# Attention with divided heads, turned logits and more sums on TensorE in a fused cross-attention and mixture-of-experts kernel

## What is computed

```python
# B, N, D = 8, 512, 512; context of M = 1601 rows; 16 heads of 32
q = qdq(layernorm(x)) @ qdq(wq).T + bq;  k, v = split(ctx @ wkv.T + bkv)
attn = softmax(q @ k.T / sqrt(32))            # per batch and head, 512 x 1601
o = attn @ v
x = x + tanh(g_xattn) * (qdq(o) @ qdq(wp).T + bp)
h = layernorm(x)
logits = h @ gate_w.T                         # 32 experts
# top 4 of the 32 within the best 2 of 4 groups, weights from sigmoid(logits), capacity 2*(N*K/E)
shared = (silu(h @ shared_gate) * (h @ shared_up)) @ shared_down
x = x + tanh(g_ffn) * (experts(h) + shared)
```

## Time and profile before

| | |
|---|---|
| median of 3 runs | 3153.32 us (3148.29 to 3154.59) |
| profiled execution | 3147.53 us, its span 3145.8 us |
| TensorE busy | 90% of the span |
| VectorE, ScalarE, GpSimd busy | 57%, 44%, 57% |
| attention | to about 2457 us of the span |
| shared FFN and routing | to about 2903 us |
| experts | the rest |

### The profile page before, as it was taken

One profiled execution on the slowest core, in us unless ns is written; L12 is line 12 of the kernel. 1 busy time (PEld: TensorE's weight loads), 2 busy tenths in 40 slices (PEclk: granted clock), 3 DMA queues, 4 the chain that ended last, 5 costly groups with the idle time before them and its releaser, 6 DMA issues. The chain is left out here.

```text
span 3145.8 us, 43433 instructions
## 1 busy us (share of the span) xinstructions
PE 2824.6 (90%) x14876; PEld 1215.4 (39%) x14876; DVE 1791.0 (57%) x3878; ACT 1383.7 (44%) x2460; POOL 1808.2 (57%) x1570
## 2 busy tenths in 40 slices
PE   5898999899989988999899899989998799998987
PEld 3333333333333333333333333333332354444766
DVE  6576567756675666667557756775664343433222
ACT  4155446644564456456545644564456210000111
POOL 0285567656656676667566656765668423223455
PEclk9798999999999999999999999999999899899999
DMA  4111012101211031103111201221011123131996
GB/s 126 39 45 52 24 35 72 54 22 35 77 53 39 18 94 47 35 22 95 30 35 58 66 23 35 72 54 33 23 53 57 68 99 110 61 121 55 310 282 116
DMA packets 146586, 215.59 MB, mean 69 GB/s; under 512 B 24984, under 2 KB 78232, under 8 KB 146368
## 3 DMA queue, kind: packets, MB, share of 16 engines
q1 hardware_dynamic: 130496, 195.95, 20.7%
q0 software_dynamic: 15872, 16.87, 2.9%
HBM read 126.49 MB, written 34.24 MB: 51 GB/s over the span
## 5 line engine op out<-in xcount | busy, mean ns | idle before, releaser
L1549 POOL TENSOR_TENSOR prob_acc<-prob_acc,probs 128x512 f32<-128x512 f32 x1152 | 1430.7, 1279 | 420.6 <-ACT probs L1065 420.6
L1065 ACT ACTIVATE probs<-s_ps 128x512 f32<-128x512 f32 (+1 forms) x1664 | 937.2, 596 | 770.0 <-PE s_ps L841 738.8
L1286 DVE TENSOR_REDUCE piece_max<-r_all 128x1 f32<-128x400 f32 (+1 forms) x2048 | 1027.7, 565 | 142.1 <-PE r_all L763 135.3
L763 PE MATMUL r_all<-k_flat,q_stack 96*128 96x400 f16 (+1 forms) x2048 | 604.7, 352 | 110.2 <-DVE piece_max L1286 41.4
L841 PE MATMUL s_ps<-q_stack,k_flat 97*128 97x512 f16 (+1 forms) x1664 | 631.1, 396 | 60.7 <-ACT probs L1065 52.5
L855 PE MATMUL o_ps<-probs,v_sb 128*32 128x512 f32 (+1 forms) x3328 | 465.3, 632 | 21.6 <-ACT probs L1065 21.6
L841 PEld LDWEIGHTS s_ps<-q_stack,k_flat 97*128 97x128 f16 (+1 forms) x1664 | 160.1, 101 | 630.5 <-ACT probs L1065 424.5
L1546 POOL COPY prob_acc<-probs 128x512 f32<-128x512 f32 x128 | 73.0, 616 | 494.1 <-PE sum_ps L875 359.5
L763 PEld LDWEIGHTS r_all<-k_flat,q_stack 96*128 96x128 f16 x2048 | 203.7, 100 | 387.7 <-DVE piece_max L1286 125.8
L1581 POOL DMA_INDIRECT slot_rows<-payload,slot x128 | 125.7, 982 | 300.1 <-DVE slot L1462 230.7
L1280 DVE SCALAR_TENSOR_TENSOR k_lo<-r_all,bk_col,k_hi 128x400 f16<-128x400 f32 (+1 forms) x128 | 81.7, 638 | 280.7 <-ACT k_hi L1023 280.7
(11 more groups left out here) (220 smaller groups left out, 2832.3 us busy)
## 6 DMA issues: line engine op xcount, KB each, us to landing
k_flat<-k_hi SPq DMA_DIRECT2D x256, 100.1 KB, 2.2
ctx_raw<-in_ctx SPq DMA_DIRECT2D x96, 256.0 KB, 2.8
xin<-in_x SPq DMA_DIRECT2D x16, 1024.0 KB, 5.6
k_flat<-k_lo SPq DMA_DIRECT2D x128, 100.1 KB, 2.2
v_sb<-in_L_ffn_w SPq DMA_DIRECT2D x18, 512.0 KB
q_stack<-q_hi SPq DMA_DIRECT2D x256, 32.0 KB, 1.8
h_rows<-work SPq DMA_DIRECT2D x8, 1024.0 KB, 4.5
x_rows<-xin SPq DMA_DIRECT2D x8, 1024.0 KB, 6.8
```

The source lines that it names most:

```text
L763: last = nc.tensor.matmul(ps[:, 0:w], q_stack[0:KSPLIT, g % 2, j, qt * P:(qt + 1) * P], k_stack[0:KSPLIT, g % 2, j, at:at + w], start=True ...
L1065: nc.scalar.activation(probs[0:w, slot, j, :], s_ps[j % SBANKS][0:w, :], ACT.Exp).then_inc(probs_ready, 1)
L1286: V.reduce_max(piece_max[:, j * TT + qt, i:i + 1], ps[:, 0:PIECE[i]], X_AXIS).then_inc(free_of(*key), 1)
L1549: last = G.tensor_tensor(prob_acc[:, j, :], prob_acc[:, j, :], probs[:, slot, j, :], ALU.add)
```

## The change

Three things change.

- **The division.** `copy_sums` and the tile `sumT` go. Behind the tiles of step 0 of the next group VectorE takes the reciprocal of `sum_ps` as it stands, 128 x 512, into `sum_sb`, and multiplies ScalarE's copy of the heads by it in place (`divide_heads`). The turn of the heads waits for that; what is turned is copied into `work` by one instruction. ScalarE's copy of the next group's heads waits until the turn of these is done.
- **The logits.** The 32 columns of the gate are the weights and the four row tiles of h move, into four strips of 32 partitions of one bank (tile `logitsT`). ScalarE copies them to SBUF, and one transpose turns them back (tile `logits`). The second down tile stands between the two.
- **The last group's sums.** TensorE sums the steps 2, 4, 6, 8, 10 and 12 of the last group, GpSimd adds the other 7.

`add_bias` stays at step 4 of g = 0. The core of the diff:

```diff
@@ -41,8 +41,8 @@
 SBANKS, NBANKS, HALVES = 2, 4, 3
-POOL_STEPS = [kt for kt in range(KT) if kt not in (4, 8, KT - 1)]
-FIRST_SUMS = 4
+PE_SUMS, LAST_PE_SUMS = (4, 8, KT - 1), (2, 4, 6, 8, 10, KT - 1)
+BIAS_STEP = 4
 MAX_STEPS = range(3, KT - 1)
@@ -74,9 +74,24 @@
+def pe_sums(n):
+
+    return PE_SUMS if n + 1 < B * GROUPS else LAST_PE_SUMS
+
+
+def pool_steps(n):
+
+    return [kt for kt in range(KT) if kt not in pe_sums(n)]
+
+
+def added_after(n):
+
+    return sum(len(pool_steps(m)) for m in range(n))
+
+
 def adds_before(s):
-    return (s // KT) * len(POOL_STEPS) + POOL_STEPS.index(s % KT)
+    return added_after(s // KT) + pool_steps(s // KT).index(s % KT)
@@ -159,8 +174,8 @@
     if f + 1 < B:
-        order += [("hT", f + 1, c) for c in range(DC)] + down[0:1] + [("logits", f + 1)]
-        down = down[1:]
+        order += [("hT", f + 1, c) for c in range(DC)] + down[0:1] + [("logitsT", f + 1)] + down[1:2] + [("logits", f + 1)]
+        down = down[2:]
     return order + down
@@ -332,6 +346,7 @@
         top8 = v_sb[:, 11, 0:TT * E].rearrange("p (t q e) -> p t q e", t=TT, q=EGROUPS)
+        logits_sb = sb("logits_sb", [P, P], FP32)
         gsum = sb("gsum", [P, TT, 8], FP32)
@@ -767,16 +783,10 @@
                 elif kind == "oT":
-                    pe.wait_ge(heads_copied, group(b, key[2]) + 1)
+                    pe.wait_ge(heads_divided, group(b, key[2]) + 1)
                     ps = open_tile(*key)
...
                         last = nc.tensor.transpose(ps[:, t * P:(t + 1) * P], oT_sb[:, t * P:(t + 1) * P], ident[:, :])
-                elif kind == "sumT":
-                    pe.wait_ge(sums_copied, group(b, key[2]) + 1)
-                    ps = open_tile(*key)
-                    for t in range(TT):
-                        last = nc.tensor.matmul(ps[:, t * GH:(t + 1) * GH], sum_sb[:, t * P:(t + 1) * P],
-                                                ident[:, ::DH], start=True, stop=True)
                 elif kind == "oiT":
@@ -795,14 +805,18 @@
                         last = nc.tensor.transpose(ps[:, t * P:(t + 1) * P], h_in[b % 2][:, t, c * P:(c + 1) * P], ident[:, :])
-                elif kind == "logits":
+                elif kind == "logitsT":
                     for c in range(DC):
...
                     ps = open_tile(*key)
-                    for t in range(TT):
-                        for c in range(DC):
-                            last = nc.tensor.matmul(ps[:, t * E:(t + 1) * E], hT[:, c, t * P:(t + 1) * P], gateT[:, c, :],
+                    for c in range(DC):
+                        for t in range(TT):
+                            last = nc.tensor.matmul(ps[t * E:(t + 1) * E, 0:P], gateT[:, c, :], hT[:, c, t * P:(t + 1) * P],
                                                     start=(c == 0), stop=(c == DC - 1))
+                elif kind == "logits":
+                    wait_read(pe, "logitsT", b)
+                    ps = open_tile(*key)
+                    last = nc.tensor.transpose(ps[:, 0:TT * E], logits_sb[:, :], ident[:, :])
                 elif kind in ("gate", "up"):
@@ -854,23 +868,24 @@
                                             probs[0:w, slot, j, :], start=(kt == 0), stop=(kt == KT - 1))
-                if kt in POOL_STEPS:
+                if kt in pool_steps(s // KT):
                     last.then_inc(probs_used, 1)
...
                 w, slot = rows(kt), s % HALVES
-                if kt == FIRST_SUMS and s >= KT:
-                    pe.wait_ge(sums_copied, s // KT)
+                first = kt == pe_sums(s // KT)[0]
+                if first and s >= KT:
+                    pe.wait_ge(sums_inverted, s // KT)
                 for j in range(GH):
                     last = nc.tensor.matmul(sum_ps[j * DH:(j + 1) * DH, :], ones[0:w, :], probs[0:w, slot, j, :],
-                                            start=(kt == FIRST_SUMS), stop=False)
+                                            start=first, stop=False)
                 last.then_inc(probs_used, 1)
...
-                pe.wait_ge(probs_added, (n + 1) * len(POOL_STEPS) * GH)
+                pe.wait_ge(probs_added, added_after(n + 1) * GH)
                 for j in range(GH):
@@ -1039,6 +1054,9 @@
                     nc.scalar.copy(hT[:, key[2], :], ps[:, :]).then_inc(free_of(*key), 1)
+                elif kind == "logitsT":
+                    ps = full(act, *key)
+                    nc.scalar.copy(logits_sb[:, :], ps[:, 0:P]).then_inc(free_of(*key), 1)
                 elif kind == "logits":
@@ -1067,12 +1085,10 @@
                 act.wait_ge(probs_used, (n + 1) * KT)
+                if n:
+                    act.wait_ge(bank_full[ring.last_bank("oT", (n - 1) // GROUPS, (n - 1) % GROUPS)],
+                                ring.done("oT", (n - 1) // GROUPS, (n - 1) % GROUPS))
                 nc.scalar.copy(oT_sb[:, :], o_ps[:, :]).then_inc(heads_copied, 1)
-
-            def copy_sums(n):
-
-                act.wait_ge(acc_summed, n + 1)
-                nc.scalar.copy(sum_sb[:, :], sum_ps[:, :]).then_inc(sums_copied, 1)
@@ -1095,8 +1111,6 @@
                         tile(key)
-                if kt == 0 and s:
-                    copy_sums(s // KT - 1)
                 if g == 2 and b + 1 < B:
@@ -1305,33 +1318,35 @@
                 po = full(dve, "oT", b, g)
-                pss = full(dve, "sumT", b, g)
-                V.reciprocal(rsum[:, :, :].rearrange("p t j -> p (t j)"), pss[:, 0:TT * GH]
-                             ).then_inc(free_of("sumT", b, g), 1)
-                wait_read(dve, "sumT", b, g)
-                for t in range(TT):
-                    last = V.tensor_tensor(
-                        work[:, t, g * P:(g + 1) * P].rearrange("p (j d) -> p j d", j=GH),
-                        po[:, t * P:(t + 1) * P].rearrange("p (j d) -> p j d", j=GH),
-                        rsum[:, t, :].unsqueeze(2).to_broadcast([P, GH, DH]), ALU.mult)
-                    if t < TT - 1:
-                        step.mark(last)
-                last.then_inc(free_of("oT", b, g), 1)
+                V.tensor_copy(work[:, :, g * P:(g + 1) * P], po[:, :].rearrange("p (t n) -> p t n", t=TT)
+                              ).then_inc(free_of("oT", b, g), 1)
                 wait_read(dve, "oT", b, g)
+
+            def divide_heads(n):
+
+                dve.wait_ge(acc_summed, n + 1)
+                V.reciprocal(sum_sb[:, :], sum_ps[:, :]).then_inc(sums_inverted, 1)
+                dve.wait_ge(sums_inverted, n + 1)
+                dve.wait_ge(heads_copied, n + 1)
+                V.tensor_tensor(oT_sb[:, :], oT_sb[:, :], sum_sb[:, :], ALU.mult).then_inc(heads_divided, 1)
...
             for b, g, kt in steps():
+                s = step_of(b, g, kt)
                 for key in lead_tiles(b, g, kt) + fill_tiles(b, g, kt):
                     tile(key)
+                if kt == 0 and s:
+                    divide_heads(s // KT - 1)
                 if g == 2 and b + 1 < B:
...
                     h_part(b - 1, kt)
+            divide_heads(B * GROUPS - 1)
             heads_out(B - 1, GROUPS - 1)
@@ -1559,9 +1574,9 @@
             for b, g, kt in steps():
-                if kt in POOL_STEPS:
+                if kt in pool_steps(group(b, g)):
                     add_probs(step_of(b, g, kt))
-                elif g == 0 and kt == FIRST_SUMS and b:
+                if g == 0 and kt == BIAS_STEP and b:
                     add_bias(b - 1)
```

More of the change, by code:

```diff
@@ L94, in head_tiles @@
 def head_tiles(b, g):
-    return [("oT", b, g), ("sumT", b, g)]
+    return [("oT", b, g)]
 def lead_tiles(b, g, kt):
@@ L179, in __init__ @@
             order += lead_tiles(*at) + fill_tiles(*at)
-        order += head_tiles(B - 1, GROUPS - 1) + [("hT", 0, c) for c in range(DC)] + [("logits", 0)]
+        order += head_tiles(B - 1, GROUPS - 1) + [("hT", 0, c) for c in range(DC)] + [("logitsT", 0), ("logits", 0)]
         for f in range(B):
@@ L319, in build @@
         prob_acc = sb("prob_acc", [P, GH, N], FP32)
-        rsum = sb("rsum", [P, TT, GH], FP32)
         hT, actT = probs[:, 0], probs[:, 1]
@@ L447, in build @@
         heads_copied = sem("heads_copied")
-        sums_copied = sem("sums_copied")
+        sums_inverted = sem("sums_inverted")
+        heads_divided = sem("heads_divided")
         h_ready = sem("h_ready")
@@ L894, in _ @@
                         heads_of(s - 1)
-                if kt and (kt - 1) not in POOL_STEPS:
+                if kt and (kt - 1) not in pool_steps(s // KT):
                     sums_of(s - 1)
@@ L902, in _ @@
             accumulated_sums(B * GROUPS - 1)
-            for key in head_tiles(B - 1, GROUPS - 1) + [("hT", 0, c) for c in range(DC)] + [("logits", 0)]:
+            for key in head_tiles(B - 1, GROUPS - 1) + [("hT", 0, c) for c in range(DC)] + [("logitsT", 0), ("logits", 0)]:
                 tile(key)
@@ L1061, in exp_of @@
                     act.wait_ge(probs_used, before + 1)
-                if before >= 0 and before % KT in POOL_STEPS:
```

(8 more changed lines are left out.)

## The result

The changed kernel takes 3200.03 us (median of 4 runs, 3198.85 to 3201.55) against 3150.81 for the kernel before: 1.0157, 95% interval 1.0135 to 1.018. It is slower, by 49 us. The profiled execution took 3198.85 us (span 3197.1), 17 us above the 3181.5 that the sum gave for it. The table has the time by stage, from the first matmul of each in the two profiles. (The last group's q tile is made at the start of the group before it, so the second stage holds two groups.)

A forecast was written before the change was run, and what follows sets the result against it. TensorE, busy 90% of the span, was taken as the bound. From the profiled 3147.5 us, +28 - 21 - 5 + 32 = +34 gave 3181.5; the forecast was 3184, range 3141 to 3212 (3168 to 3198 by itself).

The forecast's parts named there:

- the rival of 3205: Each new stand of TensorE brings its clock down to 1.2 GHz for a while: +24 us, 3205; chance 0.20.
- the two waits that it named: ScalarE's square root some 4 us later in seven groups; TensorE idle about 4.5 before each later batch's third down tile.
- The reciprocal: VectorE's reciprocal of 512 elements a partition, out of PSUM, takes 3.25 us, with a 0.69 us multiply behind it.
- The statistics behind the division: In g = 1 of batches 1 to 7 the statistics wait for the division: 4.0 us a group, +28.
- Costs nothing: In the other groups only a k_lo piece stands behind the division, covered by its DMAs' wait; uncovered, 0.8 a group.
- step 3: Attention groups: dropping the turned sums saves TensorE 1.4 us at 15 places, -21; bounds -12 and -30.
- The last group: Accumulated sums complete 7.6 us earlier, but the turn of the heads waits for the division: net -5, bounds -8 and -3.
- The logits: Shared FFN: a further bank makes TensorE stand 4.5 us in six batches, 6.3 in batch 0; less 1.6, +32.
- no gain: Logits of the six batches after batch 0: the column-tiled form's smaller weights save nothing there.
- short reciprocal: The reciprocal takes 0.7 us instead of 3.25, saving 2.55 at 7 starts and the tail: 3161; chance 0.10.
- Quick logits: Pauses vanish with smaller weight loads: 5.1 us less in six batches, perhaps the half clock too; 3131 to 3150; chance 0.24.
- Something other than the matmuls' length sets it: Shared FFN, first turn of h to second down tile: some 13 us whether the logits ran without pause or paused.

The follow-up runs named there:

- experiment 2: The changed kernel with the division placed behind the row block's statistics in VectorE's queue: 3100.46 us on chip C, 1.0003 of the kernel before.
- experiment 5: The kernel before with only the last group's new split of sums between TensorE and GpSimd: 3141.08 us on chip A, ratio 0.9978.
- experiment 8: The changed kernel without GpSimd's indirect DMAs: 3123.02 us on chip C (1.007 of the kernel before), 3123.21 us on chip B (0.9929).

## Why the prediction was right

The time (3200 in 3141 to 3212) and the sign were right, and so were the two waits that it named. The size was not: by the profiled executions the change costs 51 us for the 34 of the sum, and 3200 lies just outside the 3168 to 3198 that the forecast had by itself, towards the rival of 3205. By its steps:

1. **The reciprocal** was 3.36 us for 3.25. The slope between two small sizes of the same operation was the right guide. By the repeat count of 8 in the Trainium skill ("VectorE: DVE Perf Modes", First, the fixed hardware budget) the estimate was 4.3; the trace has 3.36, 6.6 ns an element. The multiply was 0.84 in most groups and 0.69 in the tail, where GpSimd adds nothing.
2. **The statistics behind the division.** Forecast +28, less the 1.4 of the turned sums in each of these seven groups: +18.2. Measured 425.8 to 444.3, +18.5, and experiment 2 took 27.4 us off these groups by the order alone. This step was right. "Costs nothing" for the other groups was right about the cover: in g = 2 TensorE's scores of step 3 start 20.5 us behind the group's q tile, where before it was 20.5 to 20.7, released by ScalarE in both. The wait ahead of them is 3.11 for 2.31 because the turned sums ahead of it are gone, as step 3 had said. Still, g = 2 and 3 of batches 1 to 6 together take longer than forecast: 912.8 to 919.2 us in the three profiles of the kernel before, 919.4 to 923.5 in those of the changed one. What is lost there is lost behind that wait, and in g = 2 it goes with the clock: between 50 and 60 us behind its q tile the granted clock was 0.88 to 0.97 in all 18 groups before (three profiles, six batches); after, it was 0.70 to 0.73 in ten groups, which take 80.9 to 81.3 us, and 0.92 in seven, which take 79.6 to 79.7. Why it falls there no run took apart.
3. **The turned sums**: g = 0 went from 591.5 to 586.2 in seven groups, -0.8 each for a forecast of -1.4. The wait of 0.54 is gone, and at the place itself the saving is there: in g = 0 of batch 1 the heads' matmuls before and behind it start 4.45 us apart before and 3.23 after. A part is lost again later in the group. In sum, attention came to +11.9 for +7, and that this is near is partly luck: the kernel before varies by 8 us in this stage (2344.2, 2336.7, 2336.0), the changed one by 3.5 (2356.1, 2355.6, 2352.7), and the first profile was the long one. On chip A, both kernels on the same chip, it is +18.9.
4. **The last group**: -11.3 for -5. By its parts, counted from the q tile: the accumulated sums are complete 11.3 us earlier, for 7.6, and from there to the gates it is 11.4 in both, for 2.6 more. Alone, the new split brings the sums 8.9 us earlier (8.2 at the gates, experiment 5). The term was mis-sized because it left out the logits at the tail (1.08 for 4.62, 3.1 us at the gates on chip C), and charged 2.6 for a division that for the most part lies under the load of the shared weights.
5. **The logits**: +50.5 for +32. The stand was right to a tenth, 4.56 and 6.39 for 4.5 and 6.3, and so was "no gain" from the small weights: 13.7 to 13.8 us from the first turn to the second down tile, against 12.9 to 13.6. (The 5.55 us that the text put at 1.2 GHz had a granted clock of 0.64, so not all of it was.) This is the step that failed by its size: missing in the sum were the clock behind the stand, 1.8 to 2.3 us in seven batches (some 15 us), and 0.6 between the first turn and the second down tile in each of six (3.5). The first of these was a rival of its own (*the clock pays again*, 1.7 a stand, 3205); it came out in the FFN, and should have been in the sum there: that the kernel before had full clock behind its second down tile, which ran unbroken, was no evidence for what follows a stand. In the seven groups of step 2 the sum came out without it.

The other rivals: the *short reciprocal* is out. *Quick logits* is half right, by chip: on chip C the tile takes 1.08 for 3.65 and wins 10.5 us once the bank is free. By the rule of the Trainium skill for a moving side of 32 ("TensorEngine Tiling (Array Packing)", When to Use Tiling) the estimate was 0.9; the trace has 1.08, near it. Where the pauses are, it wins nothing. "Something other than the matmuls' length sets it" was right; what it is, experiment 8 shows for chip B: GpSimd's indirect DMAs. Their sixteen of a batch lie across this stretch in every run that has them, 0.97 us each. In the changed kernel's two profiles with pauses TensorE's last one ends 1.1 to 1.3 us after GpSimd has waited for their landing and goes on, in each of the six batches (here 2583.72 against 2582.60):

```profile
2580.21 0.97 POOL L1596 DMA_INDIRECT slot_rows<-payload,slot  x1 [0.30 <-issue]
2582.60 0.20 POOL L1587 CAST payload<-token 128x16 int32<-128x16 f32 x1 [1.41 <-POOLq L1600]
```

## What to carry over

When a helper tile joins a ring of buffers, count which later tile now inherits the slot of which earlier one, and place that one's reader ahead of long work in its own queue: one moved line gave back 40 us. A long operation belongs behind the short ones on which another engine waits: the same division cost 27 us more ahead of the statistics than behind them. And price a new stand of TensorE with the clock behind it, here 4.56 + 1.8 to 2.3.

## What was not expected of the hardware

- GpSimd's indirect DMAs (16 in 20 us, 128 rows of 8 bytes each) go with slow progress of other engines on two of three chips: TensorE pauses 0.3 to 4.4 us at a time with nothing released ("issue"), ScalarE's copies come 1.3 to 3.7 us late ("remote"). In the changed kernel the stretch takes 7.4 us more in each of six batches, and the second down tile behind it 2.2 to 2.6 more for its clock. On chip B, where the DMAs were left out once, both were wholly gone; on chip A that was not tried. On chip C the same DMAs at the same places cost nothing. By what path they get in the way, and why not on every chip, is open. It is not the amount of data, and no load of instructions either: around the pauses of batch 1 the changed kernel's trace (2559 to 2600 us) has no packets but the indirect DMAs' own, 512 of them with 0.01 MB. Moving the DMAs away from the logits was not tried.
- On such a chip a faster instruction inside the stretch is worth nothing; a kernel should be compared on more than one chip before a few tenths of a per cent are believed. The same change is 1.6% slower on chip A and 1.0% slower on chip C.
- A VectorE reciprocal of 512 elements a partition takes 3.36 us, where a multiply takes 0.69.
